# Third layer's joint stage: two additions and a pair of projections per place, against one piece of each engine's mixer work per count

## What is computed

```
x_pad = jnp.pad(inputs, ((0, 0), (pl, pr), (0, 0)))
local_proj = (x_pad @ w2)[:, idx]
q = inputs @ w1
score = jnp.squeeze(jnp.tanh(local_proj + q[:, :, None, :]) @ v, -1)
weight = jax.nn.softmax(score, axis=-1)
output = jnp.einsum('btk,btkh->bth', weight, x_pad[:, idx])
```

```
for e in range(E):
    s = jnp.where(taken, -jnp.inf, scores[:, e])
    _, idx = jax.lax.top_k(s, C)
    parts.append(idx)
    taken = taken.at[idx].set(True)
```

## Time and profile before

| what | us |
|---|---|
| three runs | 2347.99, 2348.16, 2351.66 |
| median | 2348.16 |
| the profiled execution | 2353.4 |
| its span | 2351.7 |
| mean granted clock of TensorE over the span | 0.901 of full speed |
| TensorE busy in the span | 2047.0 |
| VectorE busy | 1348.8 |
| ScalarE busy | 1049.6 |
| the joint stage, from and to | 1228.5 to 1485.4 |
| of it the 56 turns | 1238.0 to 1379.8 |
| of it POOL's 32 scatters, first start to last end | 1395.2 to 1435.9 |

### The profile page before, as it was taken

The page is one execution under the profiler, slowest core; times in us unless marked ns, Lnnn a source line. Parts: engine busy times, 40 slices in busy tenths (PEclk is TensorE's granted clock), DMA queues, the critical chain, the costliest instruction groups (busy, mean ns, idle before and its releaser), DMA issues. The chain is left out here.

```text
span 2351.7 us, 46351 instructions
## 1 busy us (share of the span) xinstructions
PE 2047.0 (87%) x18079; PEld 1375.7 (59%) x18079; DVE 1348.8 (57%) x3508; ACT 1049.6 (45%) x2516; POOL 625.4 (27%) x720
## 2 busy tenths in 40 slices
PE   4989999977789999699847776858999999999898
PEld 2556666656666776454534443635666666666565
DVE  2027777734455555465348773124966767776677
ACT  3325655632244444212334334335666666666322
POOL 3016920011110000105650023362333333333100
PEclk9989999987869999799955566876999999999999
DMA  2034030021010000501240011340000000000000
GB/s 64 18 30 21 2 38 2 2 56 17 12 53 1 1 1 1 189 18 30 34 149 12 20 34 46 72 96 24 1 1 1 1 2 1 1 1 1 5 14 19
DMA packets 118327, 64.38 MB, mean 27 GB/s; under 512 B 65848, under 2 KB 113248, under 8 KB 116960
## 3 DMA queue, kind: packets, MB, share of 16 engines
q1 hardware_dynamic: 106128, 52.37, 9.6%
q0 software_dynamic: 11264, 8.66, 2.7%
q10 hardware_dynamic: 720, 0.40, 0.1%
HBM read 37.54 MB, written 23.86 MB: 26 GB/s over the span
## 5 line engine op out<-in xcount | busy, mean ns | idle before, releaser
L3000 ACT ACTIVATE l_prob<-l_ps,l_neg_max 128x128 f32<-128x128 f32 (+1 forms) x512 | 208.2, 419 | 50.0 <-DVE l_neg_max L3101 45.2
L1621 ACT ACTIVATE l0a_prob<-l0a_pst 128x1024 f32<-128x1024 f32 x128 | 131.0, 1023 | 119.9 <-PE l0a_pst L1539 119.9
L2885 POOL TENSOR_TENSOR l_prob<-l_prob,l_total 128x256 f32<-128x256 f32 x128 | 78.4, 612 | 371.8 <-DVE l_total L3109 371.8
L1672 DVE TENSOR_REDUCE l0a_peak<-l0a_ps 128x4 f32<-128x1024 f32 x128 | 156.2, 1221 | 15.5 <-PE l0a_ps L1534 13.4
L1534 PE MATMUL l0a_ps<-l0a_k,l0a_q 32*128 32x256 f32 x1024 | 146.0, 403 | 3.3 <-ACT l0a_prob L1621 2.5
L1539 PE MATMUL l0a_pst<-l0a_q,l0a_k 32*128 32x256 f32 x1024 | 145.8, 400 | 0.2 <-ACT l0a_prob L1621 0.2
L644 ACT ACTIVATE l0e_hidden<-l0e_ph,l0f_b 128x512 f32<-128x512 f32 x128 | 87.9, 687 | 129.1 <-PE l0e_ph L555 129.0
L3097 DVE TENSOR_TENSOR l_ps<-l_ps,future 128x512 f32<-128x512 f32 x128 | 89.4, 698 | 97.3 <-PE l_ps L2931 97.0
L565 PEld LDWEIGHTS l0e_py<-l0f_w,l0e_hidden 128*128 128x128 f32 x1024 | 119.7, 192 | 35.0 <-ACT l0e_hidden L644 32.8
L2886 POOL TENSOR_TENSOR l_prob<-l_prob,l_total 128x512 f32<-128x512 f32 x128 | 133.0, 1039 | 0.0
L565 PE MATMUL l0e_py<-l0f_w,l0e_hidden 128*128 128x128 f32 x1024 | 129.8, 280 | 0.3 <-ACT l0e_hidden L644 0.3
(11 more groups left out here) (518 smaller groups left out, 4833.6 us busy)
## 6 DMA issues: line engine op xcount, KB each, us to landing
l_band<-zero SPq DMA_DIRECT2D x16, 272.0 KB, 6.1
x_tok<-in_x_dram SPq DMA_DIRECT2D x2, 2048.0 KB, 7.9
l2f_w<-in_L_ffn_w_dram SPq DMA_DIRECT2D x2, 2048.0 KB, 9.8
l_rows<-l_band SPq DMA_DIRECT2D x16, 256.0 KB, 3.1
l1f_w<-in_L_ffn_W_dram SPq DMA_DIRECT2D x3, 1024.0 KB, 12.0
l2x_rows<-l2x_sent SPq DMA_DIRECT2D x8, 288.0 KB, 4.7
gd_tri<-gp_tri SPq DMA_DIRECT2D x8, 256.0 KB, 2.0
l0f_w<-gd_tri SPq DMA_DIRECT2D x8, 256.0 KB, 11.8
```

Source lines behind the costliest of these rows:

```text
L1621: act.activation(prob[:, (n // 2) % 2, pair, :, :].rearrange("p g t s -> p g (t s)"), pst[:, :, :, :].rearrange("p g t s -> p g (t s)"), A ...
L1672: dve.tensor_reduce(to, ps[m % 2][:, :, :, :], AX.X, ALU.max, negate=True).then_inc(max_ready, 1)
L3000: act.activation(prob[:, m % 4, h, cols], ps[m % 2][:, h, cols], ACT.Exp, bias=neg_max[:, m % 4, h, t:t + 1], accum_out=total[:, m % 4, h, ...
```

## The change

`SLOTS` goes. An iteration now has six beats with one turn each (`BEATS`, `slots_at(m, k)`). `add` is cut into six pieces of 3, 3, 2, 3, 3 and 2 windows (`WIDTHS`, `STARTS`), one per beat, each inside the beat's turn; `SUMMED[n]` is the number of pieces that tanh number n waits for, and the semaphore counts 6 per sequence instead of 8. On TensorE the pieces of `measure` are at beats 0, 2, 3 and 5, the projection is split, with w2's half at beat 1 and w1's at beat 4, and each comes behind the beat's count. `places` follows the last turn at once, in (9, beat 1), and so does `first_places`. `LAG` is 8 instead of 9. `turn_scores` of the last sequence is at (16, beat 1) instead of the end of iteration 16. Lines that only shift their places to new numbers (weigh at beat 2, turn_rows at beat 3, from iteration 16 on the other way round; shift and share at beat 2) complete it.

```diff
-    LAG = 9
+    LAG = 8
     PER = 8
-    SLOTS = (2, 1, 2, 1)
+    WIDTHS = (3, 3, 2, 3, 3, 2)
+    BEATS = len(WIDTHS)
+    STARTS = [sum(WIDTHS[:k]) for k in range(BEATS)]
+    SUMMED = [next(k + 1 for k in range(BEATS) if STARTS[k] + WIDTHS[k] >= KG * (n + 1)) for n in range(CHUNKS)]
...
-    CHOSEN = -(-TURNS * PER // sum(SLOTS))
+    CHOSEN = divmod(TURNS * PER - 1, BEATS)
...
                 for m in range(BATCH + LAG + 1):
-                    for n in range(CHUNKS):
-                        turns = slots_at(m, n)
-                        for e, s in turns[0:1]:
+                    for k in range(BEATS):
+                        for e, s in slots_at(m, k):
                             count_over(e, s)
-                        if n == 0 and m + 2 < BATCH:
+                        if m < BATCH and k in (0, 2, 3, 5):
+                            if k == 0 and m >= 2:
+                                pe.wait_ge(score_saved, m - 1)
+                            measure(m, (0, 2, 3, 5).index(k))
+                        if k == 1 and m + 2 < BATCH:
                             project(m + 2)
-                        if m < BATCH:
-                            if n == 0 and m >= 2:
-                                pe.wait_ge(score_saved, m - 1)
-                            measure(m, n)
-                        for e, s in turns[1:]:
-                            count_over(e, s)
-                        if n == 0 and m == CHOSEN:
+                        if k == 4 and m + 2 < BATCH:
+                            project_again(m + 2)
+                        if (m, k) == CHOSEN:
                             first_places()
-                        if n == (2 if m >= BATCH else 1) and 0 <= m - LAG - 1 < BATCH:
+                        if k == 1 and m == BATCH:
+                            turn_scores(m - 1)
+                        if k == (3 if m >= BATCH else 2) and 0 <= m - LAG - 1 < BATCH:
                             weigh(m - LAG - 1)
-                        if n == (1 if m >= BATCH else 2) and 0 <= m - LAG < BATCH:
+                        if k == (2 if m >= BATCH else 3) and 0 <= m - LAG < BATCH:
                             turn_rows(m - LAG)
-                    if 0 <= m - 1 < BATCH:
+                    if 1 <= m < BATCH:
                         turn_scores(m - 1)
...
-                    for n in range(CHUNKS):
-                        turns = slots_at(m, n)
-                        for half in range(2):
-                            mine = turns if len(turns) == 1 else turns[half:half + 1]
-                            if mine and (half == 0 or len(turns) == 2):
-                                count_front(*mine[0])
-                            if n == 0 and half == 0 and 0 <= m - 1 < BATCH:
-                                save_scores(m - 1)
-                            if m + 1 < BATCH:
-                                add(m + 1, n, half)
-                            if mine and (half == 1 or len(turns) == 2):
-                                count_back(*mine[0])
+                    for k in range(BEATS):
+                        for e, s in slots_at(m, k):
+                            count_front(e, s)
+                        if k == 0 and 0 <= m - 1 < BATCH:
+                            save_scores(m - 1)
+                        if m + 1 < BATCH:
+                            add(m + 1, k)
+                        for e, s in slots_at(m, k):
+                            count_back(e, s)
+                        if (m, k) == CHOSEN:
+                            places()
...
-                    if m == CHOSEN:
-                        places()
```

More of the change, by code:

```diff
@@ L2330, in layer2_mix_and_choose, with slots_at @@
     T = WAYS - 1
-    CHOSEN = -(-TURNS * PER // sum(SLOTS))
+    CHOSEN = divmod(TURNS * PER - 1, BEATS)
     LATE = BATCH // 2
-    def slots_at(m, n):
-        first = sum(SLOTS) * m + sum(SLOTS[:n])
-        return [divmod(k, PER) for k in range(first, first + SLOTS[n]) if k < TURNS * PER]
+    def slots_at(m, k):
+        return [divmod(BEATS * m + k, PER)] if BEATS * m + k < TURNS * PER else []
     with ExitStack() as ctx:
@@ L2426, in project, with project_again @@
                         pe.wait_ge(pq_saved, 2 * (b - 1))
-                    x = st.xnt[:, b * SEQ:(b + 1) * SEQ]
-                    pe.matmul(pp[b % 2][:, 0, :], w2[:, :], x, start=True, stop=True)
-                    pe.matmul(pp[b % 2][:, 1, :], w1[:, :], x, start=True, stop=True).then_inc(proj_ready, 1)
+                    pe.matmul(pp[b % 2][:, 0, :], w2[:, :], st.xnt[:, b * SEQ:(b + 1) * SEQ], start=True, stop=True)
+                def project_again(b):
+                    pe.matmul(pp[b % 2][:, 1, :], w1[:, :], st.xnt[:, b * SEQ:(b + 1) * SEQ], start=True, stop=True).then_inc(proj_ready, 1)
                 def measure(b, n):
@@ L2602, in _, with add @@
                 link = Chain(dve, dve_step)
-                HALF = KG // 2
-                def add(b, n, half):
-                    if n == 0:
+                def add(b, k):
+                    first, wide = STARTS[k], WIDTHS[k]
+                    if k == 0:
                         dve.wait_ge(pq_saved, 2 * (b + 1))
                     if b >= 2:
-                        dve.wait_ge(tanh_used, CHUNKS * (b - 2) + n + 1)
-                    k = n * KG + half * HALF
-                    one = padded[:, b % 2, k:k + SEQ]
-                    windows = bass.AP(one.tensor, one.offset, [one.ap[0], [1, HALF], [1, SEQ]])
-                    dve.tensor_tensor(th[:, b % 2, k:k + HALF, :], windows, q[:, b % 2, :].unsqueeze(1).to_broadcast([P, HALF, SEQ]), ALU.add)\
-                       .then_inc(sum_ready, 1)
+                        dve.wait_ge(tanh_used, CHUNKS * (b - 2) + (first + wide - 1) // KG + 1)
+                    one = padded[:, b % 2, first:first + SEQ]
+                    windows = bass.AP(one.tensor, one.offset, [one.ap[0], [1, wide], [1, SEQ]])
+                    dve.tensor_tensor(th[:, b % 2, first:first + wide, :], windows, q[:, b % 2, :].unsqueeze(1).to_broadcast([P, wide, SEQ]),
+                                      ALU.add).then_inc(sum_ready, 1)
                 def save_scores(b):
```

15 lines of the change are left out of this document (8 added, 7 removed).

## The result

The changed kernel takes 2310.07 us (median of 2308.04, 2308.28, 2311.85 and 2324.77) against 2349.91 for the kernel before on the same chip (2347.99 to 2353.48): a ratio of 0.9846, 95% interval 0.983 to 0.9861. The profiled execution took 2308.04 us, its span is 2306.2.

What follows compares the result with a forecast made beforehand. A round trip of comparison and count read-out paced the choice; then the scatter cost the loop about 30 us. -22.1 (choice, places) + 7.3 - 1 - 0.1 = -15.9: 2332 us for the median, range 2318 to 2342.

Steps and rivals of the forecast that it cites:

- Steps 1 to 3: Choice (56 turns): projection halved and moved, additions in six pieces, lag of 8; -11.6 us in sum.
- step 1: Projection halved and moved in the choice: seven dear turns fall from 3.65 to 3.87 us to 2.25, -10.8 us.
- the dear turn with turn_scores: Turn of the choice with the score copy: stays at 2.69 us, as turn_scores is still behind the last piece.
- Step 4: Places right behind the last turn, -10.5 us; POOL starts at 1373.1, with one iteration more to do, +7.3.
- one iteration more: Loop behind POOL's earlier start has one iteration more to do: +7.3 us (5.8 to 8.7).
- Step 5: Stretch behind POOL's start: 45.2 us and two iterations, as before; bounds +14.7 (no iteration done) to -30.
- nothing lost: Lower bound for the stretch behind POOL's start: the scatter costs the loop nothing, -30 us.
- rival A: Stretch gets further, as instruction supply decides: one iteration more, 2325 or 2318 us; 2302 if nothing lost. Chance 0.17, 0.03 near 2302.
- B: Rival: instruction block caught 68 instructions into the scatter, 1.5 iterations fewer, +11, so 2343 us; chance 0.05.
- C: Rival: turns of the choice don't shorten as said, +4.3 and +3.5, 2336 to 2341 us; chance 0.10.
- D: Rival: group 1's rows are stored and loaded within the slow stretch, 25 us late, 2357 us; chance 0.06.
- the toll: Slow stretch behind POOL's start taken as a fixed cost of the scatter, about 30 us, wherever it starts.

Runs made afterwards that it cites:

- the pair's chip: Chip on which the two kernels of the result ran: kernel before 2349.91 us, changed kernel 2310.07 us.
- third set: Both kernels unchanged, and each with one fill, on a chip without the slow stretch: kernel before 2314.31 us, changed kernel 2299.16 us (0.9934).
- e8_after_fill1_whole: Changed kernel with one fill behind each scatter, both projection halves in beat 1: 2306.49 us, 3.9 more than with the projection split.
- fourth set: Further runs of variants of both kernels on another chip without the slow stretch, the kernel before at 2315.15 us.
- e15_after_itself: Changed kernel, unchanged, on a chip where the kernel before took 2315.15 us: 2303.73 us, ratio 0.9948.
- e2_before_paced: Kernel before with two small fills on POOL behind each of the 32 scatters: 2328.20 us, ratio 0.9893.
- e1_before_early: Kernel before with only places() and first_places() moved right behind the last turn: 2343.67 us, ratio 0.9964.
- e18_before_early: Kernel before with only places() and first_places() right behind the last turn, on another chip with the stretch: 2346.61 us, ratio 0.9976.
- e4_after_late: Changed kernel with places() and first_places() put back to the end of iteration 10: 2332.08 us, ratio 0.9902 to the kernel before.
- e17_before_pauses: Kernel before with dense scatters and eight fills behind the 8th, 16th and 24th, on a chip with the stretch: 2330.12 us, ratio 0.9911.

## Why the prediction was wrong

The sum has three parts that can be read in one column each: choice (first turn to last), last turn to POOL's first scatter, and first scatter to the loop's last save. The pair's chip has the slow stretch, the third set's has not.

| us | choice | to the scatter | scatter to last save |
|---|---|---|---|
| before, the pair's chip | 140.85 | 16.36 | 89.76 |
| after, the pair's chip | 129.60 | 5.82 | 68.50 |
| difference | -11.25 | -10.54 | **-21.26** |
| before, third set | 141.01 | 17.35 | 51.19 |
| after, third set | 129.50 | 5.81 | 57.41 |
| difference | -11.51 | -11.54 | **+6.22** |
| forecast | -11.6 | -10.5 | +6.2 |

On the pair's chip the three sum to 43.05 us; with 1.9 by which the stage began earlier and 0.5 behind it that is the 45.4 between the two profiled executions. The third column's ends in the third set are these rows, the kernel before and then the changed one:

```profile
1391.83 1.11 POOL L2596 DMA_INDIRECT l2x_sent<-l2f_tagged,l2f_slot  x1 [166.17 <-DVE l2f_slot L2705]
...
1443.02 0.39 ACT L2546 ACTIVATE mixer_out<-l_pp 128x256 f32<-128x256 f32 x1 [0.57 <-PE l_pp L2472]
```

```profile
1373.07 1.11 POOL L2602 DMA_INDIRECT l2x_sent<-l2f_tagged,l2f_slot  x1 [142.99 <-DVE l2f_slot L2709]
...
1430.48 0.38 ACT L2552 ACTIVATE mixer_out<-l_pp 128x256 f32<-128x256 f32 x1 [0.57 <-PE l_pp L2475]
```

**Steps 1 to 3, the choice: right.** -11.6 forecast, -11.25 measured. Plain turns take 2.25 to 2.27, none is near 3.8, the dearest are 2.90. Inside step 1 the credit was misplaced: halving is worth 2.5 (e8_after_fill1_whole), which leaves the rest of the 10.8 for the moving. That the dear turn with turn_scores keeps its 2.69 was near: 2.82, since a piece of three windows stands in it.

**Step 4, the places: right.** 10.5 forecast and 10.54 measured; POOL started at 1371.49, which is within 0.3 us of 1373.1 less the 1.9 by which the stage began earlier in this execution's span. The price of one iteration more was 7.3 and is about 6.1 where the loop runs freely, within the bounds given. That the third column of the third set meets the forecast so closely is partly luck: the changed kernel, run again in the fourth set (e15_after_itself), took 60.57 us there and not 57.41, and the 7.3 came from iterations that were themselves slow.

**Step 5 failed: "taken at 45.2 us and two iterations, as before".** It took the slow stretch for a fixed toll that comes with the scatters. The runs show three things against it. In three of the six measurements of the kernel before it wasn't there. Where it is there, it goes away when POOL leaves gaps (e2_before_paced, 2353.01 to 2328.20 us). And the changed kernel escapes most of it: from first scatter to last save it loses 11.1 us (68.50 against 57.41), the kernel before 38.6 (89.76 against 51.19). The difference of 27.5 us is what the forecast missed; with the 6.2 us that it had, that makes the -21.26. The prediction had the value "nothing lost" as its lower bound for this step and gave rival A's end of it, 2302, a chance of 0.03. Rows 6 and 7 came from a single execution of one program, and nothing in them says that the cost would follow a moved scatter unchanged.

The stretch's size was wrong too. By the earlier trace rows I priced 30 us, with the iterations behind it at 7.33 each; those were still slow, as the same kernel's 6.1 us in the third set show, and the loss was 39. Wrong as well was the reading of the waits: "All of them wait for TensorE." TensorE had issued the last matmul of the save's work 18 us before the save at 1440.68, and in e1_before_early 23.4 us before the one at 1418.47.

**Rivals.** A was right in direction, its cause wrong: no block decides. B did not happen, nor C. D did not: the first row of group 1's softmax stood at 1378.12 and SP's store at 1379.06, before any late wait. The place of the prediction where the profile said most against the toll was A's own objection, that ScalarE's late waits begin long before TensorE's crawl.

**Why the changed kernel escapes.** What fits most of what the chips with the stretch show is a loop that feeds itself: while VectorE adds, POOL's issues are stretched and spaced; while they are spaced, the other engines' waits end on time, and VectorE has work. If a wait ends late, VectorE falls idle, POOL drops to 1.26 a step, and stays there nearly until the last scatter. The Trainium skill (Trainium Architecture — The Big Picture, What this means for kernel authors) says that VectorE and GpSimd contend for a shared port pair by an exclusive lock. The trace agrees as far as it goes: in the changed kernel scatters of up to 1.69 us beside additions, 0.96 without them. The changed kernel starts the scatters two iterations sooner and adds in pieces of 768 elements; neither alone was enough (e1_before_early, e18_before_early, e4_after_late). Against it speaks that in the kernel before POOL kept its 1.26 a step from 1400.71 to 1403.24 though VectorE was adding, and that in e1_before_early TensorE ran again from 1419.85 while POOL issued densely until 1423.47. On the third set's chip the dense steps had no late wait at all. So this loop is argued, from the order of events and from e2_before_paced and e17_before_pauses; VectorE's part in it was not taken away by itself. **What stays open**: what holds back the word of finished work while POOL issues densely (the profile models the ends of matmuls, so it doesn't tell a late end from a late signal), what limits TensorE to steps of 0.70 us there, why that crawl outlasts POOL's issuing by 3.8 us in the kernel before (to 1439.72), and what differs between the chips, or between their conditions at that hour; packets of the scatter took 0.10 us on the mean on either kind.

## What to carry to other kernels

Scatters that POOL issues without a gap can, on some chips, hold up TensorE, ScalarE and VectorE far beyond their own bytes. Where a trace shows late waits or an engine crawling beside them, a short fill or two behind each scatter is a cheap test (two were shown to work), and they must not make the scatters outlast the work beside them. A stretch that no resource explains is no constant: give it a range down to nothing, and as much chance for it to vanish as to stay, when its surroundings are changed. Measure on more than one chip before a gain is put down to an edit: here the same change is worth 40 us on one chip and 11 to 15 on others. And in a late wait look at when the work waited for was issued: if it was long before, more speed in that engine won't end the wait.

## What the runs showed of the hardware that was not expected

The kernel before has a median of 2350 to 2353 us in three measurements and of 2314 to 2317 in three others; none of its executions lay between 2323 and 2341 us, and a single one of 8716.76 us in the fourth set lay outside both groups. TensorE's granted clock over the first 1230 us of the span is 0.92 on either kind. The changed kernel takes 2310 and 2299 to 2304.

POOL's shortest step for a scatter of 128 rows was 1.26 us (0.96 and 0.30 between), 1.45 with one fill and 1.82 with two. Eight fills of 256 elements a partition took 2.92 us, 0.36 each.

Beside the dense scatters a wait can end 18 to 31 us after TensorE's last matmul for it (its modelled end): 18.1 us in the kernel before (save at 1440.68), 23.4 in e1_before_early (1418.47), 30.7 in e18_before_early (1432.95, last matmul ended at 1402.21).

TensorE can be held to one instruction every 0.70, 1.40, 2.10 or 2.80 us with no wait in sight, and its granted clock falls with it (0.61 in the stretch of 45.20 us). The whole choice runs at 0.50 in the changed kernel and at 0.59 in the kernel before, though TensorE is busy for a larger share of it in the changed one: 115.75 of 129.60 us against 106.19 of 140.00.
